# Down projection of a graph layer's experts as seven products of halves

## The reference, cut to what matters

```python
weights = _routing_weights(x, Wr, temperature)          # 8 experts, softly weighted
gate = jnp.einsum('btd,edi->beti', x, Wg)
up = jnp.einsum('btd,edi->beti', x, Wu)
h = jax.nn.silu(gate) * up                               # 8 x 128 hidden features
e_out = jnp.einsum('beti,eid->betd', h, Wd)
out = jnp.einsum('bte,betd->btd', weights, e_out)
...
x = x + _L0_ffn_ref(_layernorm(x, axis=-1)[None], ...)[0]
```

## Time and profile before

| | |
|---|---|
| median of 3 runs | 1101.61 us (1101.35 to 1101.86) |
| the profiled execution | 1102.07 us, its span 1100.1 us |
| TensorE busy | 1089.3 us, 99% |
| VectorE, ScalarE, GpSimd busy | 34%, 23%, 27% |
| experts | about 765 to 988 us from the start of the span |
| down projection | 987.7 to 1096.8 us |

### The profile page before, as it was taken

The page is one execution under the profiler, slowest core; times in us unless marked ns, Lnnn a source line. Parts: engine busy times, 40 slices in busy tenths (PEclk is TensorE's granted clock), DMA queues, the critical chain, the costliest instruction groups (busy, mean ns, idle before and its releaser), DMA issues.

```text
span 1100.1 us, 15031 instructions
## 1 busy us (share of the span) xinstructions
PE 1089.3 (99%) x5647; PEld 903.7 (82%) x5647; DVE 374.4 (34%) x996; ACT 251.4 (23%) x398; POOL 294.0 (27%) x243
## 2 busy tenths in 40 slices
PE   8999999999999999999999999999999999999998
PEld 7887778887888888888788888887788888888887
DVE  6944656675631111322211223444321111111111
ACT  5320211121232344211111113334131111112000
POOL 4000011121141356300054445343142222235000
PEclk9999999999999999999999999999999999999999
DMA  7203012222243586504199987764032222215321
GB/s 266 96 29 106 13 35 59 67 70 67 66 146 119 188 287 218 187 1 153 42 277 322 292 234 204 232 190 140 1 87 62 62 62 62 74 59 212 115 96 67
DMA packets 145977, 139.28 MB, mean 127 GB/s; under 512 B 7958, under 2 KB 115826, under 8 KB 145650
## 3 DMA queue, kind: packets, MB, share of 16 engines
q1 hardware_dynamic: 145330, 136.48, 39.7%
q10 hardware_dynamic: 576, 1.84, 0.5%
HBM read 102.32 MB, written 35.96 MB: 126 GB/s over the span
## 4 chain that ended last, share of the span: by engine, by line
PE 95%; DVE 3%; DMA 1%; ACT 1%; issue 1%; SPq 0%; ACTq 0%; DVEq 0%
PE ps L1590 9%; PE ps L1592 9%; PE ps L1591 9%; PE ps L1890 7%; PE ps L1891 7%; PE ps L1892 7%; PE ps L1831 4%; PE ps L1825 4%; PE ps L1805 3%; PE ps L1756 3%; PE ps L1807 3%; PE ps L1806 3%; PE ps L1938 3%; PE ps L1939 3%; PE ps L1758 3%; PE ps L1940 3%
## 5 line engine op out<-in xcount | busy, mean ns | idle before, releaser
L1590 PE MATMUL ps<-w_hi,xnH 128*128 128x512 f32 x464 | 184.6, 398 | 0.0
L1592 PE MATMUL ps<-w_hi,xnL 128*128 128x512 f32 x464 | 180.9, 390 | 0.0
L1591 PE MATMUL ps<-w_lo,xnH 128*128 128x512 f32 x464 | 180.7, 389 | 0.0
L736 POOL TENSOR_TENSOR acc<-acc,cw 128x320 f32<-128x320 f32 x40 | 35.8, 894 | 252.6 <-ACT cw L920 251.5
L1590 PEld LDWEIGHTS ps<-w_hi,xnH 128*128 128x128 f32 x464 | 87.1, 188 | 18.7
L1592 PEld LDWEIGHTS ps<-w_hi,xnL 128*128 128x128 f32 x464 | 87.1, 188 | 18.5
L1591 PEld LDWEIGHTS ps<-w_lo,xnH 128*128 128x128 f32 x464 | 87.2, 188 | 17.2
L1543 DVE TENSOR_TENSOR prd<-ps,wB 128x512 f32<-128x512 f32 (+1 forms) x24 | 14.2, 592 | 161.9 <-PE ps L1892 147.8
L1756 PE MATMUL ps<-xnH,w_hi 128*128 128x512 f32 (+1 forms) x192 | 68.1, 355 | 0.0
L1890 PE MATMUL ps<-x2H,guH 128*128 128x512 f32 (+1 forms) x192 | 67.7, 352 | 0.4 <-ACT wT L1100 0.4
L1891 PE MATMUL ps<-x2L,guH 128*128 128x512 f32 (+1 forms) x192 | 67.6, 352 | 0.0
(11 more groups left out here) (316 smaller groups left out, 2068.7 us busy)
## 6 DMA issues: line engine op xcount, KB each, us to landing
cR<-c_d SPq DMA_DIRECT2D x20, 640.0 KB, 5.0
foldin<-in SPq DMA_DIRECT2D x32, 256.0 KB, 2.7
guR<-in SPq DMA_DIRECT2D x16, 512.0 KB, 5.4
w_raw<-in SPq DMA_DIRECT2D x14, 512.0 KB, 6.7
c_d<-cw SPq DMA_DIRECT2D x40, 160.0 KB
qs0H<-qT_d SPq DMA_DIRECT2D x10, 512.0 KB, 5.3
qs0L<-qT_d SPq DMA_DIRECT2D x10, 512.0 KB, 6.6
ob<-x_d SPq DMA_DIRECT2D x20, 256.0 KB, 2.7
```

The costliest lines, as they stand in the source:

```text
L1590: pe.matmul(target, xnH[:, kc, cols], wH[w][:, kc, :], start=(kc == 0), stop=False)
L1591: pe.matmul(target, xnH[:, kc, cols], wL[w][:, kc, :], start=False, stop=False)
L1592: mm = pe.matmul(target, xnL[:, kc, cols], wH[w][:, kc, :], start=False, stop=(kc == KC - 1))
```

## The change

The hidden layer (tokens x 1024) is cut into halves of 5 token tiles and 4 experts, Wd into halves of 4 experts and 512 columns, and the four quarters of the result are made from seven products (q = 0 to 6) of sums of such halves instead of eight. Each product is 5 tiles (r) of 4 x 3 matmuls. The low precision parts of h are no longer made in the expert steps: h is kept whole in f32 (`hT`), and each 128 x 512 operand of the left side is summed and split just ahead of its product into one of three rooms (`hxH`, `hxL`), by ScalarE and VectorE. The seven panels of the right side are made while the experts run: five loads of quarters of Wd and one repeated one, four mixed panels on GpSimd, seven high parts on ScalarE and seven low parts on GpSimd. Two panels (q = 0, 1) stay in the core's memory, five are stored in DRAM (`wd_d`) and read back after the last expert. Sums of products are kept in `u2` and `u3`, which GpSimd adds into x; `ob` has twelve rooms. Some semaphores are merged (z_step into rt, x1_sqrt into ln_sqrt, deg_st and in_deg into deg_way).

```diff
 # SP, the expert steps
             for n in range(24):
-                if n == 23:
-                    load_d0(0)
                 load_wb(n)
                 e = n // 3
                 if n % 3 == 2 and e + 2 < NEXP:
                     load_gu(e + 2)
+                if n == 1:
+                    load_down(0, 1, 1, 0)
+                    load_down(1, 0, 1, 1)
+                if n == 6:
+                    store_down(0, 0)
+                    store_down(0, 1)
+                if n == 7:
+                    store_down(1, 0)
+                if n == 8:
+                    store_down(1, 1)
+                    sp.wait_ge(wd_st[0], 32)
+                    load_down(2, 0, 0, 2)
+                if n == 10:
+                    store_down(2, 0)
+                    store_down(2, 1)
+                if n == 12:
+                    store_down(3, 0)
+                    store_down(3, 1)
+                    load_down(0, 1, 0, 3)
+                if n == 14:
+                    store_down(4, 0)
+                    store_down(4, 1)
+                    load_down(1, 0, 0, 4)
+                if n == 15:
+                    sp.wait_ge(wd_st[1], 80)
+                    load_down(3, 1, 0, 5)
...
+            def load_down(k, rows_half, cols_half, landing):
+                source = wd_pan[cols_half].rearrange("q (k n) -> q k n", n=W)[:, 4 * rows_half:4 * rows_half + 4, :]
+                sp.dma_start(wdq[k][:], source).then_inc(in_d[landing // 5], 16)
+
+            def store_down(k, part):
+                sp.wait_ge((wd_hi, wd_lo)[part], k + 1)
+                sp.dma_start(wd_d[MADE[k] - 2, part], (wdH, wdL)[part][1][:].bitcast(F32)).then_inc(wd_st[part], 16)
...
+            sp.wait_ge(up_mm, 3 * NEXP)
             for k in range(3):
                 sp.wait_ge(x1_st[k], 16 * (8, 6, 6)[k])
+            sp.wait_ge(wd_st[0], 80)
+            load_panel_of(2)
+            for n in range(4):
+                load_o(n)
+            for q in range(3, 7):
+                load_panel_of(q)
             for d in range(2 * NT):
-                hf, t = d // NT, d % NT
+                hf, t = down_out(d)
+                if d == HALF:
+                    sp.wait_ge(d_mm, 2 * HALF)
+                    for n in (5, 6):
+                        load_o(n)
...
                 sp.wait_ge(d_dr, d + 1)
-                sp.dma_start(out[t][:, hf * W:(hf + 1) * W], ob[:, d % 4, :]).then_inc(o_st[d % 4], 16)
-                if d + 4 < 2 * NT:
-                    load_o(d + 4)
+                sp.dma_start(out[t][:, hf * W:(hf + 1) * W], ob(d)).then_inc(o_st[d % 4], 16)
+                if d == 0:
+                    sp.wait_ge(o_st[0], 16)
+                    load_o(4)
...
 # GpSimd
+            def mixed_panel(k):
+                first, second, target, op = ((0, 1, 1, ALU.subtract), (1, 2, 1, ALU.add), (0, 1, 0, ALU.subtract),
+                                             (0, 1, 1, ALU.subtract))[k]
+                if k != 2:
+                    pool.wait_ge(in_d[0], 16 * (2, 3, 3, 4)[k])
+                pool.tensor_tensor(wdq[target][:], wdq[first][:], wdq[second][:], op).then_inc(wd_mix, 1)
+
+            def panel_low(k):
+                source, high, low = ((0, 1, 1), (1, 1, 1), (1, 1, 1), (0, 1, 1), (1, 1, 1), (1, 0, 0), (3, 1, 1))[k]
+                pool.wait_ge(wd_hi, k + 1)
+                if 1 <= k < 5:
+                    pool.wait_ge(wd_st[1], 16 * k)
+                if k:
+                    pool.wait_ge(wd_mix, (0, 1, 2, 3, 4, 4, 4)[k])
+                pool.tensor_tensor(wdL[low][:], wdq[source][:], wdH[high][:].bitcast(F32), ALU.subtract).then_inc(wd_lo, 1)
...
             for e in range(2):
                 gu_low(e)
-            for n in range(24):
...
-                hidden_low(n)
-                if c == 2 and e + 2 < NEXP:
-                    gu_low(e + 2)
-                if n == 21:
-                    down_low(0)
...
+            mixed_panel(0)
+            panel_low(0)
+            gu_low(2)
+            panel_low(1)
+            mixed_panel(1)
+            gu_low(3)
+            panel_low(2)
+            mixed_panel(2)
+            gu_low(4)
+            panel_low(3)
+            mixed_panel(3)
+            panel_low(4)
+            gu_low(5)
+            panel_low(5)
+            panel_low(6)
+            for e in (6, 7):
+                gu_low(e)
...
+            for d in range(HALF, 2 * NT):
+                add_earlier(d)
 # ScalarE
+                if n in (3, 4, 6, 8, 10, 12, 13):
+                    panel_high((3, 4, 6, 8, 10, 12, 13).index(n))
+                if n in (20, 21):
+                    token_high(n - 20)
...
+            for i in range(2, 7 * HALF):
+                token_high(i)
+                if 3 <= i < 3 + HALF:
+                    first_product_out(i - 3)
 # VectorE
+            for i in range(2, 7 * HALF + 3):
+                if i < 7 * HALF:
+                    token_low(i)
+                if i >= 3:
+                    product_out(i - 3)
+                if 4 <= i < 4 + HALF:
+                    first_sums(i - 4)
+                if 9 <= i < 9 + HALF:
+                    third_sum(i - 9)
+                if 18 <= i < 18 + HALF:
+                    fourth_sum(i - 18)
 # TensorE
+                for k in range(4):
+                    hi, lo = hxH[i % 3][:, k, :], hxL[i % 3][:, k, :]
+                    high, low = wdH[q][:, k, :], wdL[q][:, k, :]
+                    pe.matmul(target, hi, high, start=(opens and k == 0), stop=False, skip_group_check=not opens)
+                    pe.matmul(target, hi, low, start=False, stop=False, skip_group_check=not opens)
+                    mm = pe.matmul(target, lo, high, start=False, stop=(k == 3), skip_group_check=not opens)
+                mm.then_inc(d_mm, 1)
```

More of the change, by code:

```diff
@@ L43 @@
 FIRST_WIN_STEP = NT + 1
+HALF = NT // 2
 CHUNKS = ((0, 512), (512, 1024), (1024, 1250))
@@ L235, in x2L, with tokens, hx_source, ob @@
             return x2L0[:, kc, :] if kc < 4 else xnL[:, kc, :]
[L237 to L240, removed]
+        def tokens(k, t):
+            return hT[k][:, :, t * P:(t + 1) * P]
+        def hx_source(i):
+            q, r = divmod(i, HALF)
+            return (lambda: tokens(0, r), lambda: tokens(1, r), lambda: hs2[:, r], lambda: tokens(0, r + HALF),
+                    lambda: tokens(1, r + HALF), lambda: hs1[:, r], lambda: tokens(1, r))[q]()
+        O_LOADS = ((0, 1, 0), (1, 2, 1), (2, 3, 2), (3, 4, 3), (4, 5, 0), (5, 10, 4), (10, 13, 9), (13, 14, 1),
+                   (14, 15, 2), (15, 16, 3), (16, 17, 0), (17, 20, 4))
+        O_LANDING = (0, 1, 2, 3, 0, 4, 5, 1, 2, 3, 0, 4)
+        def ob(d):
+            first, last, room = next(load for load in O_LOADS if load[0] <= d < load[1])
+            room += d - first
+            return ob_few[:, room, :] if room < 4 else ob_many[:, room - 4, :]
+        def ob_in(d):
+            n = next(n for n, load in enumerate(O_LOADS) if load[0] <= d < load[1])
+            return in_o[O_LANDING[n]], 16 * O_LANDING[:n + 1].count(O_LANDING[n])
+        MADE = (6, 3, 2, 5, 4, 0, 1)
+        def down_out(d):
+            return (0, d) if d < NT else (1, (d - HALF) % NT)
         ps = nc.alloc_psum_tensor("ps", [P, 8 * BANK], F32)
@@ L283, in gps_layer @@
         in_gu = [[sem(f"in_gu{k}_{g}") for g in range(2)] for k in range(2)]
-        in_d = [sem(f"in_d{k}") for k in range(6)]
-        in_o = [sem(f"in_o{k}") for k in range(4)]
+        in_d = [sem(f"in_d{k}") for k in range(2)]
+        wd_st = [sem(f"wd_st_{part}") for part in ("hi", "lo")]
+        in_wd = [sem(f"in_wd{q}") for q in ("2", "3", "4_to_6")]
+        in_o = [sem(f"in_o{k}") for k in range(6)]
         o_st = [sem(f"o_st{k}") for k in range(4)]
@@ new lines, in _, with load_o @@
+                if n == 15:
+                    sp.wait_ge(wd_st[1], 80)
+                    load_down(3, 1, 0, 5)
+            def load_o(n):
+                (first, last, room), (hf, t) = O_LOADS[n], down_out(O_LOADS[n][0])
+                target = ob_few[:, room, :] if room < 4 else ob_many[:, room - 4:room - 4 + last - first, :]
+                source = x1_d[t:t + last - first, :, hf * W:(hf + 1) * W].rearrange("t q n -> q t n")
+                sp.dma_start(target if room >= 4 else target.unsqueeze(1), source).then_inc(in_o[O_LANDING[n]], 16)
@@ L671, in _, with load_panel_of @@
+            def load_panel_of(q):
+                for part in range(2):
+                    sp.dma_start((wdH, wdL)[part][q][:].bitcast(F32), wd_d[q - 2, part]).then_inc(in_wd[min(q - 2, 2)], 16)
+            sp.wait_ge(up_mm, 3 * NEXP)
             for k in range(3):
                 sp.wait_ge(x1_st[k], 16 * (8, 6, 6)[k])
[L673 to L677, removed]
@@ L844, in _ @@
-            down_low(1)
-            down_low(2)
+            pool.wait_ge(a_done, 2 * NT)
+            for k in range(2):
+                pool.memset(hT[k][:, :, N:NP], 0.0).then_inc(pads, 1)
+            mixed_panel(0)
```

(49 more changed lines are left out.)

235 lines of the change are left out of this document (142 added, 93 removed).

## The result

The changed kernel takes 1116.13 us (median of 4 runs, 1114.38 to 1117.78) against 1101.68: a ratio of 1.0132, 95% interval 1.0118 to 1.0145, slower. The forecast was 1110.0 with a range up to 1116.0; the direction and the place were right, the size was 6 us short, and the time lies just outside the range. The profiled execution is the fastest of the four, 1114.38 with a span of 1112.3.

What follows compares the result with a forecast made beforehand. TensorE, busy for 99% of the span, was taken as the bound. Terms: -13.6 (fewer matmuls) +18.1 (wait ahead of n=9) +0.9 (ahead of n=15) +2.0 (clock) +1.0 (product 13) = +8.4, giving 1110.0 us, range 1104 to 1116.

Steps and rivals of the forecast that it cites:

- The saving: Down projection: seven products instead of eight remove 60 matmuls of 0.2268 us each, 13.6 us less.
- the main wait: Ahead of n=9 (expert 3): TensorE idles 18.1 us for gu_low(3), behind mixed_panel(1) and its late third load.
- The slower outcome: Whole kernel: the change makes it slower than before; chance 0.90.
- slow transfers: Rival: read-back panels and other transfers run at 3.4 us per MB, lengthening all waits; 1116 to 1126 us; chance 0.08.
- short wait: Rival: transfers share the engines (wait ahead of n=9 13.7 us) or the clock loses nothing; 1103 to 1105; chance 0.08.
- the small terms: Waits beside the long one: 0 ahead of n=6, 0.9 us ahead of n=15, 1.0 us near product 13.
- Ahead of n=15: Start of expert 5: fourth load, mix 3 and low 4 delay gu_low(5); TensorE waits 0.9 us, bounds 0 and 3.7.
- gu_low(2) ends about 0.5 us ahead of n=6: Start of expert 2: gu_low(2) is ready in time, no loss; 0.6 us if transfers are a fifth slower.
- Product 13: Down stage: first store queues behind panel read-backs, delaying load_o(4) and VectorE; TensorE waits 1.0 us, bounds 0 and 10.5.
- the term of the clock: After the wait ahead of n=9: TensorE falls to 1.2 GHz for a stretch, costing 2.0 us, bounds 0 and 2.9.

Runs made afterwards that it cites:

- all orders: Changed kernel with each gu_low on GpSimd ahead of neighbouring panel work, ScalarE's high 4 at n=11, panels 4 to 6 read back after load_o(4): 1087.98 us.
- two exchanged lines: Changed kernel with gu_low(3) ahead of mixed_panel(1) on GpSimd instead of behind it: 1099.24 us, ratio to before 0.9975.

## Why the prediction was right in kind and short in size

*Right.* The saving (13.6; the version with all orders returns 13.8). The place, mechanism and size of the main wait: 18.1 forecast and 18.1 measured, each link within 0.5 us, and the order of the queue with it. That what the change gives is lost to order and not to load: shown by two exchanged lines, and by all orders together. The slower outcome, forecast at 0.90. The *slow transfers* rival (1116 to 1126) is where the median fell by its number, but its mechanism is not what happened: it had the load land some 12.6 us after n=8, and it landed after 11.3; and panels 3 to 6 came back at 2.7 us per MB, not at 3.4. That the range of this rival held the result is luck. The *short wait* rival has its own sum wrong: a wait of 13.7 with the other terms gives +2 to +4, not +0.9 to +3, and with the wait at 18.1 and no loss of clock it is +6.4.

*Wrong: the small terms, each too small.* This is the step that failed, with 4.1 of the missing 6.1 us. The mechanisms were right (each wait came where it was named or where its reserve was called thin), the sizes were not: together the terms beside the long wait and the clock were forecast at 1.9 us and measured at 6.0 in the profiled execution.
- Ahead of n=15, "0.9 us", 2.9 measured. The fourth load landed 15.7 us after the end of n=11, not 14.0, and TensorE was let go 2.9 us after gu_low(5) began, not 2.4 (its two halves took 5.62 us, not 4.8; VectorE was at its products meanwhile, but no run separates that cause). Two stretches with reserves of tenths of a us can't both be taken at the mean rate.
- "gu_low(2) ends about 0.5 us ahead of n=6": guR landed at 813.24 and 814.71, 1.4 us later than worked out; 0.7 us of loss.
- Product 13, "1.0 us", 2.4: the store was held 13.9 us and the load behind it came at 35.7 us after the experts' end, not 34.8. By my own steps the sum was 1.5, and I rounded down.

*Wrong: the term of the clock.* "After the long wait I expect a fall to 1.2 GHz and such a stretch again ... I take 2.0": in the profiled execution 1.6, so the step looked right; in the other profiled executions with that wait it was 2.5 and 3.2, the second above the bound of 2.9. And I put the clock at one place alone. It also fell after waits of 2.05, 2.51, 2.69, 2.80 and 3.35 us, in some executions, at 1.7 to 1.9 us each where the loss of expert 5 shows it. I put the 1.75 us by which the median is above the profile down to this; the runs' mean clocks say so, the unprofiled runs have no waits to look at. Of the missing 6.1 us, the small waits are 4.1, the start of the experts, 0.2 us later than before, 0.2, the clock 1.35 (1.75 more, less the 0.4 by which the profiled fall was cheaper than forecast), and 0.5 is that I took the median to lie below the profiled execution, as it did before.

## What to carry to other kernels

Where engines run a written order, put what a consumer is due to wait for ahead of what merely fills time, and for each filling instruction ask which release its own data hangs on: here a load behind a wait for the end of step n=8 stood ahead of what step n=9 needed. Add up busy time and you see 52 us of GpSimd in 220 and no problem; follow each wait through SP's order and you see 18. When several small reserves are within a us of nothing, forecast their sum at the slow end of the rows, and give every wait of TensorE of 2 us or more a chance of costing the clock as well, some 1.7 to 1.9 us each time here.

## What the runs showed of the hardware

- After a wait of 18.1 us TensorE's granted clock was at 0.50 and matmuls of 128x512 went at 0.43 us instead of 0.23. It was also at 0.50 after waits of 2.05, 2.51, 2.69, 2.80, 3.35 and 4.62 us (after the 2.51 and the 3.35 only 0.8 and 1.5 us after a restart at the full pace), and not after waits of 2.10, 2.17, 2.61 and 2.98 us: the length of the wait alone does not decide it. The same kernel's runs ranged over 3.6 us with it. Useless matmuls in the wait made the kernel 4.7 us faster, of which, in the profiled executions, 1.35 us are a load that landed sooner.
- VectorE's splits and sums of two SBUF operands (128x512) grew from 0.69 to as much as 1.77 us while GpSimd added two SBUF operands, whose own additions grew from 1.29 to 1.75 us; with GpSimd's work shrunk to one column they were 0.69 again. Additions that read PSUM stayed at 0.68 throughout.
- A store of 256 KB that landed in 2.0 us on a free queue took 13.9 us behind what was left of 10 MB of loads issued by the same engine before it.
